# Rotary work in two jobs per tile, and full-height local queries, in an eight-stage two-layer network

## The chip, the cores and the metric

The kernel runs on one core of one Trainium2 chip. The metric is the device time of the whole program in microseconds (us). The engines are TensorE (PE, with its weight loads shown apart as PEld), VectorE (DVE), ScalarE (ACT), GpSimd (POOL) and SyncE (SP), which here only issues DMAs. A change of less than 0.2% (10 us) is about what a measurement of this kernel can not tell from none.

## What is computed

A residual stream x of shape (8, 512, 256), float32, goes through eight sublayers, each on the layer-normalised stream and added back: differential attention, mixture of experts, routed (local plus selected) attention, experts again, a selective state space, a block-quantised feed-forward, full attention, the same feed-forward. Two of them matter here.

```python
# differential attention, 16 half-heads of 16 channels, causal
q, k = rotary(rmsnorm(x @ Wq)), rotary(rmsnorm(x @ Wk))   # x1*c + x2*s, -x1*s + x2*c
att = softmax(q1 k1.T) v - lam * softmax(q2 k2.T) v       # per head, then a layernorm per head
y = ((1 - lam_init) * layernorm(att)) @ Wproj
# routed attention: 8 heads of 64 channels
light = softmax(mask + q_local @ k_window.T) v             # windows of 64 keys, three to a query
heavy = softmax(hq @ hk.T) hv                               # 256 picked queries, 256 picked keys
y = light @ wo_l + scatter(heavy @ wo_h)
```

## The kernel before

**Differential attention** (`diff_attention`, L143). The work is one software pipeline over 128 slots: 16 half-heads (NH) in each of 8 batches (B). Every engine walks the same slot numbers in program order; semaphores tie them together. In slot s PE computes the scores of softmax s+2 (L264, stationary operand 48 rows high), in even slots the values of a finished pair (L279, output in two 64-column halves), and then whatever "odd" jobs the hand-written `table` (L156) puts there: transposing x, projecting q and k (`qk`) and v, turning q and k (`turn`, L307), turning a head's output back (`back`), turning the attended rows (`heads`) and the output projection (`out`). A table entry (at, kind, i) is slot 16 b + at for batch b, so -17 is slot 15 of an earlier batch's sixteen. Odd jobs share three PSUM banks (NODD) in order; a bank must be emptied by ACT or DVE before the third next job may fill it. `vector_table`, `scalar_table` and `pool_table` (L160 to L166) place the jobs of the other engines; an engine empties in slot s what PE filled in slot s-1, before its own table jobs.

The rotary work of a tile t is one DVE job, `rope` (L477): multiply the 128x512 tile by the reciprocal norm (L478), drain and signal, wait for POOL's `swap` (L562) which multiplies the swapped halves with the sine (L569), multiply by the cosine in place (L482), drain, add POOL's half (L486). A `turn` job waits for all four tiles of its batch (L308), transposes four blocks (L310); ACT rounds the result to `hi` (L385), DVE subtracts to `lo` (L428), both in two buffers; ACT waits for the spill of the chunk two before (L384). SP writes hi and lo to DRAM with six DMAs a chunk (L245), four chunks a batch, and then issues some 20 DMAs of 512 KB that clear DRAM for the experts (`clear_regions`, L2734). POOL's `stack` jobs (L573, slots -9 and -1) wait for the spill and load it back into qT and kT, which the scores read. POOL also multiplies the causal triangle into each softmax (L546, L548). ACT computes the exponentials (L346), and once per batch two square roots, which need table loads.

When a head is done (`back` on DVE, L431 to L445), DVE takes the reciprocals of the eight row sums (L435), multiplies four of them by -lambda (L437), multiplies both halves (L438, L440) and adds them (L445), with a drain after each step.

**Routed attention** (`routed_attention`, L1134) is the same kind of pipeline over 192 slots: 8 batches, 4 chunks of two heads, 4 light and 2 heavy softmaxes a chunk. `scores` (L1233): for a light one a bf16 matmul adds the mask to the bank (L1242), then two matmuls of 256 columns (L1254) contract 64 rows, partitions 0 to 63 or 64 to 127 by the head's parity `par`, of q and k (L1249, L1250) or of the tile hqk (L1252, L1253). Then come `turn` (four transposes of the softmax of slot s-1, L1265), in every second slot `values` (L1291), and odd jobs in two banks. ACT copies q and k out of PSUM (L1447) and both halves of hqk in one copy (L1452), each releasing its bank after a drain. Before the pipeline a prologue on DVE (L1577 to L1600) sets constants and signals `s_ready`, on which POOL and PE wait.

## Time and profile before

| what | before |
|---|---|
| median of 3 runs | 4904.13 us (4897.9 to 4906.65) |
| the profiled execution | 4896.55 us |
| its span, first to last instruction | 4894.8 us |
| PE busy in the span | 3919.6 us (80%) |
| DVE / ACT / POOL busy | 2934.8 / 1749.0 / 1554.0 us |
| mean granted PE clock | 0.892 of full |
| differential attention, about | 35 to 670 us |
| routed attention, about | 1250 to 2108 us |

The profiled execution's own time exceeds its span by 1.75 us; it lies 7.6 us (0.15%) below the median of the runs. Busy time is the union of an engine's instructions; ends of matmuls are modelled, so the distance from one start to the next says more than a duration does. A float32 matmul shows as two records.

### The profile page before, as it was taken

How to read it: one execution, taken by the hardware profiler on the slowest of the kernel's cores; microseconds unless marked ns; L12 is line 12 of the kernel's file. 1: busy time of each engine (PE TensorE's matmuls, PEld its weight loads, DVE VectorE, ACT ScalarE, POOL GpSimd, SP SyncE). 2: the span in 40 equal slices, each digit the busy share in tenths (PEclk: the TensorE clock that was granted, in tenths of full speed). 3: DMA queues.
4: the chain of work that ended last, by engine and by line, in shares of the span. 5: the costliest groups of instructions: out<-in, count | busy, mean ns of one | idle time of the engine just before them, and what ended most of it. 6: DMA issues, size and time to landing. Idle time of an engine off the chain costs nothing. (4 is left out here: it accounts for less than half of the span.)

```text
span 4894.8 us, 59730 instructions
## 1 busy us (share of the span) xinstructions
PE 3919.6 (80%) x19240; PEld 2599.4 (53%) x19240; DVE 2934.8 (60%) x5538; ACT 1749.0 (36%) x3490; POOL 1554.0 (32%) x1463
## 2 busy tenths in 40 slices
PE   2888877994599999987993677774887788888888
PEld 2555556883477777766883334342554233333555
DVE  4566656664544445456664556556897466664898
ACT  2555543441344443443441232322111255545111
POOL 2555525445555444435445000000000433430000
PEclk7898988997799999988997788887998699998999
DMA  4988902553100000002554100000000544440000
GB/s 123 262 215 240 260 24 84 163 170 114 34 1 1 1 1 1 1 28 89 165 165 141 32 0 0 0 0 13 0 0 1 108 88 94 92 91 14 9 13 13
DMA packets 222619, 348.69 MB, mean 71 GB/s; under 512 B 34136, under 2 KB 127258, under 8 KB 216218
## 3 DMA queue, kind: packets, MB, share of 16 engines
q1 hardware_dynamic: 199706, 261.27, 17.7%
q0 software_dynamic: 22656, 84.24, 7.9%
q8 instruction: 131, 2.15, 0.2%
q14 instruction: 126, 1.03, 0.1%
HBM read 166.90 MB, written 169.87 MB: 69 GB/s over the span
## 5 line engine op out<-in xcount | busy, mean ns | idle before, releaser
L2532 DVE TENSOR_REDUCE ab_nmx<-banks 128x1 f32<-128x512 f32 x512 | 334.9, 687 | 226.8 <-PE banks L2348 226.0
L2586 POOL DMA_DIRECT2D ab_kT<-in_ab_ones x4 | 2.1, 535 | 1072.6 <-POOLq L2737 1072.6
L1620 POOL TENSOR_TENSOR lb_pq<-lb_pq,lb_rr 128x512 f32<-128x512 f32 x192 | 201.6, 1053 | 424.1 <-DVE lb_rr L1519 421.5
L2474 ACT ACTIVATE ab_pt<-banks 128x512 f32<-128x512 f32 x512 | 273.8, 600 | 94.8 <-PE banks L2358 83.0
L1514 DVE TENSOR_REDUCE lb_nmx<-banks 128x2 f32<-128x512 f32 x192 | 132.1, 688 | 278.1 <-PE banks L1254 277.1
L1402 ACT ACTIVATE lb_pq<-banks,lb_nmx 128x256 f32<-128x256 f32 x384 | 178.9, 471 | 301.0 <-DVE lb_nmx L1514 300.9
L2358 PE MATMUL banks<-ab_qT,ab_kT 49*128 49x512 f32 x512 | 232.1, 501 | 56.5 <-ACT ab_pt L2474 51.7
L2348 PE MATMUL banks<-ab_kT,ab_qT 48*128 48x512 f32 x512 | 239.6, 517 | 30.3 <-DMA ab_kT<-ab_spill 19.2
L2358 PEld LDWEIGHTS banks<-ab_qT,ab_kT 49*128 49x128 f32 x512 | 94.1, 198 | 271.9 <-ACT ab_pt L2474 158.7
L279 PE MATMUL banks<-da_pt,da_vx 128*64 128x512 f32 (+3 forms) x1024 | 183.5, 508 | 0.0
L346 ACT ACTIVATE da_pt<-banks 128x512 f32<-128x512 f32 (+1 forms) x384 | 174.9, 535 | 13.7 <-PE banks L264 12.6
L264 PE MATMUL banks<-da_qT,da_kT 48*128 48x512 f32 (+3 forms) x512 | 132.2, 377 | 40.9 <-ACT da_pt L346 32.1
L546 POOL TENSOR_TENSOR da_pt<-da_pt,w_da_tri 128x384 f32<-128x384 f32 x128 | 133.8, 1045 | 77.3 <-ACT da_pt L346 76.9
L1000 DVE CAST moe_a_h_hi<-moe_a_h_raw 128x512 fp32r<-128x512 f32 x124 | 88.6, 714 | 112.9 <-ACT moe_a_h_raw L873 112.0
L2369 PE MATMUL banks<-ab_pt,ab_vx 128*32 128x512 f32 x1024 | 152.7, 672 | 0.0
L1000 DVE CAST moe_b_h_hi<-moe_b_h_raw 128x512 fp32r<-128x512 f32 x124 | 85.8, 692 | 110.5 <-ACT moe_b_h_raw L873 109.6
L1084 POOL TENSOR_TENSOR moe_a_w_lo<-moe_a_w_raw,moe_a_w_hi 128x1024 fp32r<-128x1024 f32 x48 | 115.7, 2415 | 114.5 <-ACT moe_a_w_hi L880 106.8
L1084 POOL TENSOR_TENSOR moe_b_w_lo<-moe_b_w_raw,moe_b_w_hi 128x1024 fp32r<-128x1024 f32 x48 | 115.6, 2413 | 102.3 <-ACT moe_b_w_hi L880 94.9
L138 PE MATMUL banks<-moe_b_w_hi,moe_b_h_hi 128*128 128x256 f32 x496 | 143.8, 290 | 3.2 <-DVE residual L1029 3.2
L138 PE MATMUL banks<-moe_a_w_hi,moe_a_h_hi 128*128 128x256 f32 x496 | 143.7, 290 | 3.2 <-DVE residual L1029 3.2
L1254 PE MATMUL banks<-lb_k,lb_q 64*128 64x256 f32 x512 | 144.3, 402 | 0.0
L138 PE MATMUL banks<-moe_b_w_lo,moe_b_h_hi 128*128 128x256 f32 x496 | 141.5, 285 | 0.0
(534 smaller groups left out, 11347.9 us busy)
## 6 DMA issues: line engine op xcount, KB each, us to landing
moe_xs<-zero SPq DMA_DIRECT2D x71, 512.0 KB, 11.0
moe_ys<-zero SPq DMA_DIRECT2D x71, 512.0 KB, 11.8
moe_a_w_raw<-in_moe_w SPq DMA_DIRECT2D x48, 512.0 KB, 3.7
moe_b_w_raw<-in_moe_w SPq DMA_DIRECT2D x48, 512.0 KB, 3.7
da_spill<-da_hi SPq DMA_DIRECT2D x128, 128.0 KB, 2.4
ab_spill<-ab_hi SPq DMA_DIRECT2D x128, 128.0 KB, 2.4
da_qT<-da_spill POOLq DMA_DIRECT2D x32, 384.0 KB, 6.9
da_kT<-da_spill POOLq DMA_DIRECT2D x32, 384.0 KB, 10.6
```

The lines of the kernel that those rows point to most:

```text
L138: done = core.nc.tensor.matmul(bank, a[i], b[j], start=(first and n == 0), stop=(last and n == len(terms) - 1))
L279: last = nc.tensor.matmul(ps[64 * sub:64 * sub + 64, AV_BANK + hv % 2, j * P:T], vx[b % 2][:, j, h, :], pt[:, (2 * hv + sub) % RING, c0:c0 ...
L346: nc.scalar.activation(pt[:, n % RING, c0:c1], ps[:, S_BANK + (3 * n + u) % 3, 0:c1 - c0], ACT.Exp, scale=1.0 / math.sqrt(DA_D)).then_inc( ...
L1000: nc.vector.tensor_copy(h_parts[0][:, n % 2, m, :], h_raw[:, m % 2, :])
L1084: nc.gpsimd.tensor_tensor(parts[1][:, l % 2, :, :], raw[:, :, :], parts[0][:, l % 2, :, :].bitcast(F32), ALU.subtract).then_inc(done, 1)
L1402: nc.scalar.activation(pq[:, n % RING, t, :], ps[:, S_BANK + n % 2, 2 * P * t:2 * P * t + 2 * P], ACT.Exp, bias=nmx[:, n % RING, t:t + 1], ...
L1620: nc.gpsimd.tensor_tensor(pq[:, n % RING, :, :], pq[:, n % RING, :, :], bcast(rr[:, n % RING, :], 2, 2 * P), ALU.mult).then_inc(s_p, 1)
L2348: nc.tensor.matmul(ps[:, MAX_BANK + n % 3, :], qT[b % 2][r:r + AB_ROWS, p, qt * P:(qt + 1) * P], kT[b % 2][r:r + AB_ROWS, p, :], start=Tru ...
L2358: nc.tensor.matmul(ps[:, EXP_BANK + n % 3, :], kT[b % 2][r:r + AB_ROWS + 1, p, j * P:(j + 1) * P], qT[b % 2][r:r + AB_ROWS + 1, p, :], sta ...
L2369: last = nc.tensor.matmul(ps[32 * i:32 * i + 32, SUM_BANK, :], vx[b % 2][:, j, h + i, :], pt[:, (4 * v + i) % RING, :], start=(j == 0), st ...
L2474: nc.scalar.activation(pt[:, s % RING, :], ps[:, EXP_BANK + s % 3, :], ACT.Exp, scale=AB_D ** -0.5).then_inc(s_e, 1)
L2532: nc.vector.tensor_reduce(nmx[:, g % 2, col:col + 1], ps[:, MAX_BANK + n % 3, :], op=ALU.max, axis=AX.X, negate=True).then_inc(s_mx, 1)
```

## The change

In differential attention the `rope` job is split: `scaled` holds the first multiplication and signals POOL without a drain, `rope` the rest. Tiles 0 and 1 are scaled in slot -20, tiles 2 and 3 in -19, the `rope` jobs lie in slots -18 and -17, the swaps one slot later than before for three of the tiles. The v projections move one slot earlier and ahead of the turns; the turns move to slots -14, -13, -12, -11, one in each. In `back` the small multiplication with -lambda and a drain go, and the last sum becomes t2 * (-lambda) + t1 in one instruction. In routed attention q and the picked queries get a copy per head parity, whose other 64 partitions are zero; the score matmuls contract all 128 partitions.

```diff
-             (-17, "turn", 0), (-16, "turn", 1), (-15, "v", 0), (-14, "turn", 2), (-14, "v", 1), (-13, "turn", 3),
+             (-16, "v", 0), (-15, "v", 1), (-14, "turn", 0), (-13, "turn", 1), (-12, "turn", 2), (-11, "turn", 3),
...
-                    (-20, "rms", 0), (-20, "rope", 0), (-19, "rope", 1), (-19, "rope", 2), (-18, "rope", 3),
+                    (-20, "rms", 0), (-20, "scaled", 0), (-20, "scaled", 1), (-19, "scaled", 2), (-19, "scaled", 3),
+                    (-18, "rope", 0), (-18, "rope", 1), (-17, "rope", 2), (-17, "rope", 3),
...
-                  (-20, "swap", 0), (-19, "swap", 1), (-19, "swap", 2), (-18, "swap", 3),
+                  (-19, "swap", 0), (-19, "swap", 1), (-18, "swap", 2), (-17, "swap", 3),
...
-                        nc.vector.tensor_scalar(rr[:, r, :, 1:2], rr[:, r, :, 1:2], nlam[:, :], None, ALU.mult)
                         nc.vector.tensor_tensor(t1[:, :, :], sums[:, :, 0, 0:32], bcast(rr[:, r, :, 0], 2, 32), ALU.mult)
-                        dve.drain()
...
-                        nc.vector.tensor_tensor(att[:, b % 2, :, i, :], t1[:, :, :], t2[:, :, :], ALU.add)
+                        nc.vector.scalar_tensor_tensor(att[:, b % 2, :, i, :], t2[:, :, :], nlam[:, :], t1[:, :, :],
+                                                       ALU.mult, ALU.add)
...
+                def scaled(b, t):
+                    nc.vector.tensor_tensor(groups(qk[:, t, :]), groups(qk[:, t, :]),
+                                            bcast(srcp[:, t, :].rearrange("p (c r) -> p c r", r=4), 2, DA_D), ALU.mult).then_inc(s_qn, 1)
+
                 def rope(b, t):
-                    nc.vector.tensor_tensor(groups(qk[:, t, :]), groups(qk[:, t, :]),
-                                            bcast(srcp[:, t, :].rearrange("p (c r) -> p c r", r=4), 2, DA_D), ALU.mult)
-                    dve.drain().then_inc(s_qn, 1)
                     dve.wait_ge(s_swap, NT * b + t + 1)
...
-        q, k = sb("q", [P, 2, T]), sb("k", [P, 2, LB_TP])
+        q, k = sb("q", [P, 2, 2, T]), sb("k", [P, 2, LB_TP])
...
-        hqk = sb("hqk", [P, 2, 2, LB_SEL])
+        hq, hk = sb("hq", [P, 2, 2, LB_SEL]), sb("hk", [P, 2, LB_SEL])
...
-                            mine = q[r0:r0 + LB_D, c, qt * P:qt * P + P]
-                            keys = k[r0:r0 + LB_D, c, qt * P:qt * P + 2 * P]
+                            mine = q[:, c, par, qt * P:qt * P + P]
+                            keys = k[:, c, qt * P:qt * P + 2 * P]
                         else:
-                            mine = hqk[r0:r0 + LB_D, c, 0, t * P:t * P + P]
-                            keys = hqk[r0:r0 + LB_D, c, 1, :]
+                            mine = hq[:, c, par, t * P:t * P + P]
+                            keys = hk[:, c, :]
...
-                        dst = q[:, chunk % 2, :] if kind == "q" else k[:, chunk % 2, LB_W:LB_W + T]
-                        nc.scalar.copy(dst, bank).then_inc(s_qk, 1)
+                        if kind == "q":
+                            nc.scalar.copy(q[0:LB_D, chunk % 2, 0, :], bank[0:LB_D, :])
+                            nc.scalar.copy(q[LB_D:P, chunk % 2, 1, :], bank[LB_D:P, :]).then_inc(s_qk, 1)
+                        else:
+                            nc.scalar.copy(k[:, chunk % 2, LB_W:LB_W + T], bank).then_inc(s_qk, 1)
...
-                        nc.scalar.copy(hqk[:, chunk % 2, :, :],
-                                       bank.rearrange("p (r n) -> p r n", r=2)).then_inc(s_hqk, 1)
+                        nc.scalar.copy(hq[0:LB_D, chunk % 2, 0, :], bank[0:LB_D, 0:LB_SEL])
+                        nc.scalar.copy(hq[LB_D:P, chunk % 2, 1, :], bank[LB_D:P, 0:LB_SEL])
+                        nc.scalar.copy(hk[:, chunk % 2, :], bank[:, LB_SEL:2 * LB_SEL]).then_inc(s_hqk, 1)
...
+                for x in (q, hq):
+                    nc.vector.memset(x[LB_D:P, :, 0, :], 0.0)
+                    nc.vector.memset(x[0:LB_D, :, 1, :], 0.0)
```

## Rows read from the trace of the kernel before

**Rows 1.** Busy time by stretch: length, then busy us per engine, PE clock, DMA, GB/s

```profile
120.00:590.00 470.00, 403.46 (x2144) 250.34 (x2143) 292.78 (x527) 251.22 (x507) 261.00 (x335) 0.88 0.88 245
1296.00:2108.00 812.00, 808.19 (x4671) 587.42 (x4671) 389.05 (x893) 353.21 (x1055) 384.39 (x340) 1.00 0.00 1
```

**Rows 2.** Waits of PE, 35 to 665 us: us in total, times, longest

```profile
PE banks L310 <- DVE da_qk L486: 66.0, 8, 20.6
```

**Rows 3.** Timeline of PE, one batch of differential attention: start, length

```profile
255.61 1.08 PE L310 MATMUL banks<-ident,da_qk 128*128 128x128 f32 x4 [5.69 <-DVE da_qk L486]
...
264.36 0.90 PE L264 MATMUL banks<-da_qT,da_kT 48*128 48x512 f32 x4
...
265.60 0.36 PE L138 MATMUL banks<-da_wv_hi,da_xT_hi 128*128 128x256 f32 x1
...
267.20 0.91 PE L264 MATMUL banks<-da_qT,da_kT 48*128 48x512 f32 x4
268.04 2.38 PE L279 MATMUL banks<-da_pt,da_vx 128*64 128x512 f32 x16
```

**Rows 4.** Timeline of DVE and POOL around the rotary work of one batch

```profile
306.87 0.69 DVE L478 TENSOR_TENSOR da_qk<-da_qk,da_srcp 128x512 f32<-128x512 f32 x1
...
307.67 1.26 POOL L569 TENSOR_TENSOR da_rot<-da_qk,w_da_sin 128x512 f32<-128x512 f32 x1 [6.79 <-DVEq L480]
...
308.89 1.00 POOL L546 TENSOR_TENSOR da_pt<-da_pt,w_da_tri 128x384 f32<-128x384 f32 x1
308.96 1.47 DVE L482 TENSOR_TENSOR da_qk<-da_qk,w_da_cos 128x512 f32<-128x512 f32 x1 [1.41 <-POOL da_rot L569]
...
324.77 3.19 DVE L112 TENSOR_SCALAR x_normed<-residual,mean_var,rstd 128x256 f32<-128x256 f32 x4
```

**Rows 5.** The first batch: PE timeline, and first issue of POOL's loads

```profile
74.06 1.94 PE L310 MATMUL banks<-ident,da_qk 128*128 128x128 f32 x8 [20.65 <-DVE da_qk L486]
...
105.69 3.10 PE L264 MATMUL banks<-da_qT,da_kT 48*128 48x512 f32 x8 [8.70 <-DMA da_kT<-da_spill]
...
L580 POOL DMA_DIRECT2D da_qT<-da_spill x32: 506/542/714, 93.3 to 585.9; - x32
```

**Rows 6.** SP's spill issues, first and last of 24, and time to landing

```profile
76.52 0.51 SPq L245 DMA_DIRECT2D da_spill<-da_hi  x1
...
91.17 0.60 SPq L245 DMA_DIRECT2D da_spill<-da_lo  x1
...
DMA to landing us min/median/max: 2.2/2.4/4.1
```

**Rows 7.** The small multiplication on DVE: duration ns min/median/max

```profile
L437 DVE TENSOR_SCALAR da_rr<-da_rr,da_nlam x64: 229/264/2057, 144.3 to 645.3; 128x4 f32<-128x4 f32 x64
```

**Rows 8.** Timeline of PE in routed attention, around one light score

```profile
1600.08 0.39 PE L1242 MATMUL banks<-lb_maskb,lb_identb 128*128 128x512 bf16 x1
1600.40 1.13 PE L1254 MATMUL banks<-lb_k,lb_q 64*128 64x256 f32 x4
1601.45 0.66 PE L1265 MATMUL banks<-ident,lb_pq 128*128 128x128 f32 x4
1601.87 0.47 PE L138 MATMUL banks<-lb_xT_hi,lb_wqkv_hi 128*128 128x512 f32 x1
1602.18 0.39 PE L138 MATMUL banks<-lb_xT_lo,lb_wqkv_hi 128*128 128x512 f32 x1
1602.41 0.39 PE L138 MATMUL banks<-lb_xT_hi,lb_wqkv_lo 128*128 128x512 f32 x1
...
1618.19 1.03 PE L1347 MATMUL banks<-lb_gT,w_lb_wkvh 128*128 128x256 f32 x4
1619.06 0.38 PE L1242 MATMUL banks<-lb_maskb,lb_identb 128*128 128x512 bf16 x1
```

**Rows 9.** DVE in the prologue of routed attention

```profile
1253.77 0.30 DVE L1587 MEMSET lb_k<- 128x128 f32 x2
```

**Rows 10.** ACT's copies of q: duration ns min/median/max, first and last start

```profile
L1447 ACT COPY lb_q<-banks x32: 586/586/589, 1289.1 to 2079.5; 128x512 f32<-128x512 f32 x32
```

More of the change, by code:

```diff
@@ L515, in rescale @@
                     nc.vector.tensor_tensor(heads_of(b), heads_of(b), bcast(mean[:, :], 2, 32), ALU.mult).then_inc(s_ln, 1)
-                jobs_of = {"normal": normal, "xlo": low_x, "sum": sum_squares, "rms": rms, "rope": rope,
+                jobs_of = {"normal": normal, "xlo": low_x, "sum": sum_squares, "rms": rms, "scaled": scaled, "rope": rope,
                            "mean": mean_of, "centre": centre, "square": square, "var": variance, "scale": rescale}
@@ L1234, in scores @@
                     b, m, kind, i, par = of(n)
-                    r0, c = LB_D * par, (LB_FC * b + m) % 2
+                    c = (LB_FC * b + m) % 2
                     bank = ps[:, S_BANK + n % 2, :]
```

## The prediction

> **What bounds the kernel now.** I read the busy time by stretch first, because the change touches two of eight stages and an average over 4.9 ms says nothing about either. In routed attention PE is busy 808.2 of 812 us at full clock, while DVE, ACT and POOL are each below half [rows 1]. Whatever PE does there is paid in full, and only PE counts. In differential attention PE is busy 403 of 470 us in the steady part, at a mean clock of 0.88, with DVE at 293, POOL at 261 and ACT at 251 [rows 1]: no engine is full, so waits decide. The list of PE's waits names the largest, the first turn of each batch on the last rotary addition: 66.0 us in 8 times, 20.6 of it in the first batch [rows 2]. So 45.4 us belong to seven later batches, 6.5 us each. The timeline of one such batch shows the cost behind the wait: from the turn at 255.61 to the scores of the next slot at 264.36 PE needs 8.75 us [rows 3].
>
> **Routed attention, the score matmuls.** The change removes no column of work; what can go is the time around the 64-row matmuls. I read start to start. The mask starts at 1600.08 and the scores at 1600.40, 0.32 us; a matmul of the same 512 columns between full-height neighbours takes 0.23 (1602.18 to 1602.41). The scores to the transposes take 1.05 us; the same columns at full height take 0.87 (1618.19 to 1619.06). The transposes to the projection and on to its second matmul take 0.42 + 0.31, where the 0.31 would be 0.23. Lost: 0.09 + 0.18 + 0.08 = 0.35 us a score [rows 8]. A matmul at full height takes no longer per column, since the 0.87 is measured at 128 rows. There are 192 scores. Those that follow `values` directly, whose output lies in 64-column halves, keep part of the loss, so I take 0.33 us: 192 x 0.33 = 63 us gained. Bounds: 0.18, if only the step after the scores goes (35 us), and 0.36 (69 us). In the Trainium skill, TensorEngine Tiling (Array Packing), under Key Properties, a change of tiling mode drains TensorE; the gaps in the rows stand where such a change would be, so by that rule the loss goes, as summed. The other way, the page TensorE: Matmul & The Clock Gate, under Part 3, has small matmuls in distinct row groups run at the same time, which zeros would forfeit; by it the change would lose where two such neighbours stand. In this kernel both matmuls of a slot lie in the same row group and the other head's come a slot later, so nothing is forfeited.
>
> **Its side costs.** Four memsets, two of 1024 and two of 512 elements a partition, join DVE's prologue, where DVE runs without a pause up to the ready signal. Two memsets of 128 take 0.30 us together [rows 9], 1.17 ns an element; 3072 elements give 3.6 us, less for start-up: I take +3 us, bounds 0 and +4. ACT gets a second copy of q (586 ns, [rows 10]) and three shorter copies in place of the one of hqk, each shorter than 586: at most 32 x (0.59 + 2 x 0.59) = 56 us on an engine that is busy 353 of 812 [rows 1]. I cost it at nothing: PE has another bank to fill meanwhile, and exponentials are waited for two slots later. If that cover goes, each late bank costs up to 0.6 us; 64 of them bound it at +38, and I keep +10.
>
> **Differential attention, the steady part.** In the new order PE does in slots 0 and 1 what needs no rotary result (output projection, v), and turns only from slot 2 on. What is late next? DVE. Splitting the job looks as if POOL's swap (1.26 us) would now run beside DVE's multiplications. The rows speak against it: the cosine multiplication that starts while POOL's triangle runs takes 1.47 us, where the multiplication of the same shape at 306.87, with POOL still, takes 0.69. It ends 0.54 us after the triangle, so it stood still for most of it [rows 4]. I therefore leave the rotary chain as long as it is, 306.87 to 324.77, plus 3.2 for the normalisation that ends at 327.96 [rows 4]. The Trainium skill, SBUF — State Buffer, holds the port pair of DVE and GpSimd to be an exclusive lock, also for a VectorE operation with two SBUF inputs; that agrees, and a forecast with full overlap would put the chain near 12 us in place of 17.9.
>
> PE fills v's first half into the bank that DVE frees after its jobs of slot 15. Let T be the time at which PE now starts the turn, after standing for 5.7 us [rows 3]. It will fill these with scores (0.9), values (2.4, [rows 3]) and an output projection (four float32 matmuls of 256 columns, 2 x 0.87 [rows 8]): 5.0 us, so PE arrives at about T - 0.7. DVE now ends the normalisation at T + 3 [rows 4]; with fewer waits in between I give it T - 0.5 to T + 2.5 and take T + 1. With v at 1.6 us (265.60 to 267.20) the next slot starts at T + 2.6, against T + 8.75 [rows 3]. The work left behind differs by 0.5 us in favour of the new order. That is 6.6 us gained a batch, bounds 4 and 8.5.
>
> Something is given back. The turns now stand in four slots in a row and pass through two hi/lo buffers. SP issues a chunk's six DMAs in (91.77 - 76.52) / 4 = 3.8 us, and they land after 2.4 [rows 6]; with ACT's and DVE's 1.3 us that is 7.5 us from turn 0 until ACT may round turn 2. Slots 3 and 4 hold little, about 5.4 us. ACT stands there, with the exponentials queued behind it and PE's scores waiting for them. I take 2 us a batch, bounds 0 and 5. POOL's load job in slot -9 has still two slots to spare. The swaps one slot later wait for what DVE has by then done, so POOL's triangles lose nothing. SP starts its clearing DMAs about two slots later; it waits longer than that before each batch's first chunk. Sum: 7 x (6.6 - 2) = 32 us gained, bounds 0 and 60.
>
> **The first batch.** There the chain to the first scores is bare: turns at 74.06, POOL's loads at 93.3, scores at 105.69 [rows 5]. The v projections and x of the next batch no longer stand behind ACT's wait for the first spill, so that the next batch's qk, which POOL's square and with it the loads are queued behind, comes earlier. The walk: first spill issued at about 75.6 (a little earlier than 76.5), second chunk landed 2 x 3.8 + 2.4 later, at 85.6 [rows 6]; ACT then rounds turn 3 (0.6) and copies the first qk, which PE has ready by then, POOL squares it (1.1), and with the signals between them the loads go out at about 88.5, against 93.3. That is 5 us gained, bounds 0 and 9.
>
> **The second softmax's factor.** 64 small multiplications of 264 ns (up to 2057 beside POOL) and 64 drains go [rows 7], 17 us by the median. DVE waits for PE's `back` most of the time, so it is worth nothing on the path, at most 5 us; the fused sum replaces one of equal size.
>
> **Sum.** -63 + 3 - 32 - 5 = -97. Against the profiled execution, 4896.55, that is 4799.5. That execution lies 7.6 us under the median of 4904.13; splitting the difference, **I predict 4804 us**.
>
> **The rivals.**
> *A, the clustered turns and the DVE/POOL exclusion eat the whole gain of differential attention's steady part.* For it: the 7.5 us against 5.4, and the 1.47 us cosine [rows 4, 6]. Against it: PE need not wait for the rotary work at all in slots 15 and 0. Time: -63 + 3 - 5 = -65, 4832, with the same offset 4836. Chance 0.12. The lock of the SBUF page is the reason such a case has a chance at all.
> *B, full-height matmuls don't remove the gaps* (they come from loading float32 weights, not from the height; the change then doesn't do what it says). For it: after the v halves a first float32 matmul is slow too. Against it: full-height scores would stand between full-height neighbours, and 0.87 is measured there [rows 8]. Time: +3 - 37 = -34, 4866. Chance 0.08.
> *C, slower.* ACT's wait for the spill two chunks back grows, because the DMA queue still carries clearing traffic (DMA busy 0.88, [rows 1]) when the denser turns come; exponentials and scores stall. Everything else sums to -63 + 3 - 46 - 5 = -111, so it decides from 111 / 7 = 16 us a batch; at 18 us a batch the time is 4916. Against it: landings are 2.2 to 4.1 us even now [rows 6]. Chance 0.03, with 0.01 for other slow ends.
> *The forecast's case* has 0.73, and 0.03 is left for sums near zero.
>
> **Range and chances.** The bounds of the forecast's own case give -134 (69 + 60 + 9 less 4) to about -45; cutting the ends that need every bound at once, and reaching to rival A, I give 4768 to 4848. A change of 0.2% (10 us) is about what the measurement can tell. Faster: 0.73 + 0.12 + 0.08 = 0.93; same 0.03; slower 0.04.
>
> **What would show it.** Right: PE's wait at L310 for the rotary addition gone but for the first batch; in routed attention scores to transposes 0.87 us, mask to scores near 0.23, the stage about 60 us shorter with PE still full; the rotary chain on DVE no shorter than 17 us. Wrong: PE waiting at v (L138) or at the scores for ACT (L346) by more than 4 us a batch; the 1.05 us unchanged at 128 rows; ACT or a bank release appearing among PE's waits of routed attention.

## The result and the profile after

The changed kernel takes 4814.13 us (median of 4 runs, 4808.16 to 4830.99), the kernel before beside it 4903.94: a ratio of 0.9827, 95% interval 0.9815 to 0.984. The forecast was 4804 in a range of 4768 to 4848. The profiled execution is the longest of the four, 4830.99 us, so stages are compared here and totals by the medians.

| stage, by its first and last instruction | before | after | difference | forecast |
|---|---|---|---|---|
| start to first differential scores | 105.7 | 98.3 | -7.4 | -5 |
| first to last differential scores | 524.5 | 507.8 | -16.7 | -32 |
| routed set-up, DVE's first write of lb_s (L1579) to first row maximum | 44.3 | 47.4 | +3.1 | +3 |
| routed attention, first to last row maximum | 810.8 | 748.9 | -61.9 | -63 |
| full attention, not touched, first to last exponential | 629.6 | 643.4 | +13.8 | 0 |

The set-up is measured from an instruction of DVE's prologue that lies ahead of the memsets and of the ready signal, so the memsets are in it. The last row is no effect of the change: in the twelve profiles below, all with the same code in that stage, it took 617.3 to 640.0 us, and the time goes with the granted clock there, 0.90 on average in this profile and 0.94 in the one of 617.3 us. It explains most of why this one profile is longer than its kernel's median.

Busy time by stretch of the changed kernel (length, busy us per engine, TensorE clock, DMA share, GB/s), the stretches moved with the stages:

```profile
120.00:573.00 453.00, 392.93 (x2105) 250.62 (x2101) 281.27 (x475) 241.55 (x491) 267.28 (x328) 0.89 0.88 252
1267.00:2020.00 753.00, 741.85 (x4628) 613.28 (x4690) 382.45 (x887) 385.87 (x1145) 381.71 (x340) 1.00 0.00 1
```

Against [rows 1] routed attention is shorter with PE still full (741.9 of 753) and still at a granted clock of 1.00, while ACT rose only to 386 of 753: PE bounds the stage as before and simply has less to do. The weight loads rose from 587 to 613 us although the stretch shrank. The steady differential stretch looks the same as before.

In routed attention, the timeline of PE around one light and one heavy score:

```profile
1599.97 0.60 PE L1266 MATMUL banks<-ident,lb_pq 128*128 128x128 f32 x4
1600.33 0.36 PE L138 MATMUL banks<-lb_wqkv_hi,lb_xT_hi 128*128 128x256 f32 x1
...
1602.49 1.03 PE L1255 MATMUL banks<-lb_k,lb_q 128*128 128x256 f32 x4
1603.35 0.60 PE L1266 MATMUL banks<-ident,lb_pq 128*128 128x128 f32 x4
...
1619.96 1.03 PE L1255 MATMUL banks<-lb_hk,lb_hq 128*128 128x256 f32 x4
1620.82 0.60 PE L1266 MATMUL banks<-ident,lb_pq 128*128 128x128 f32 x4
```

Scores to transposes, start to start, is 0.86 us in both; it was 1.05 [rows 8], and the medians over 189 scores are 0.86 and 1.06. The transposes to the next work take 0.36 in place of 0.42, and a mask to its scores 0.22 (1652.50 to 1652.72) in place of 0.32. Same columns, same clock, less time around them.

In differential attention the waits of PE from 0 to 700 us (us in total, times, longest):

```profile
PE banks L265 <- ACT da_pt L347: 31.2, 21, 3.1
PE banks L138 <- DVE residual L448: 25.0, 5, 5.3
PE banks L311 <- DVE da_qk L487: 15.3, 1, 15.3
...
PE banks L138 <- DVE da_t L439: 6.1, 1, 6.1
```

The 66.0 us at the turn [rows 2] are down to 15.3, all in the first batch. In its place PE waits at the v projection: 25.0 + 6.1 us in six of the seven later batches. So 45.4 us of later waits became 31.1. The timeline of PE, POOL and DVE in the batch around 300 us says why:

```profile
294.09 1.05 POOL L581 DMA_DIRECT2D da_qT<-da_spill  x2
295.14 1.00 POOL L581 DMA_DIRECT2D da_kT<-da_spill  x2
296.15 1.28 POOL L570 TENSOR_TENSOR da_rot<-da_qk,w_da_sin 128x512 f32<-128x512 f32 x1
296.88 1.99 PE L327 MATMUL banks<-w_da_wo,x_normed_T 128*128 128x256 f32 x8
297.39 1.00 POOL L547 TENSOR_TENSOR da_pt<-da_pt,w_da_tri 128x384 f32<-128x384 f32 x1
297.47 3.23 DVE L483 TENSOR_TENSOR da_qk<-da_qk,w_da_cos 128x512 f32<-128x512 f32 x1 [2.78 <-POOL da_rot L570]
...
303.45 0.68 DVE L448 TENSOR_TENSOR residual<-banks,residual 128x512 f32<-128x512 f32 x1
...
304.19 0.58 PE L138 MATMUL banks<-da_wv_hi,da_xT_hi 128*128 128x256 f32 x1 [5.31 <-DVE residual L448]
```

PE ends the output projection at 298.87 and waits 5.31 us for the bank that L448 frees. DVE is late because its last cosine waits 2.78 us for POOL's last swap, and the swap stands behind the four load issues of the "stack" jobs, 2.05 us together (0.5 each), in the slot to which the change moved it. The cosine then takes 3.23 us, with POOL's triangles beside it. And after the wait v runs slowly, 2.86 us from 304.19 to the next scores at 307.05, where it took 1.6 in [rows 3].

The whole rotary chain of that batch, from DVE's first scaling to its last addition, is the second measure of this. DVE's timeline, the changed kernel first, then loads_late (an experiment below, with those load issues one slot later):

```profile
281.84 4.97 DVE L478 TENSOR_TENSOR da_qk<-da_qk,da_srcp 128x512 f32<-128x512 f32 x4
...
300.78 1.32 DVE L487 TENSOR_TENSOR da_qk<-da_qk,da_rot 128x512 f32<-128x512 f32 x1
```

```profile
279.83 4.96 DVE L478 TENSOR_TENSOR da_qk<-da_qk,da_srcp 128x512 f32<-128x512 f32 x4
...
295.97 0.79 DVE L487 TENSOR_TENSOR da_qk<-da_qk,da_rot 128x512 f32<-128x512 f32 x1
```

That is 20.3 us in the changed kernel and 16.9 in loads_late; before it was 18.0 (306.87 to 324.85). In the fourth to the eighth batch it is 17.9 to 18.0 us in the two profiles with the code of before, 20.2 to 21.1 in the five of the changed code, and 16.3 to 17.4 in the three with the change and the later loads. So the change made the chain over 2 us longer.

Three short stretches of the same profile show the clock:

```profile
295.00:300.00 5.00, 3.88 (x24) 2.30 (x20) 2.53 (x1) 0.70 (x2) 4.98 (x8) 1.00 1.12 351
...
307.00:310.00 3.00, 3.00 (x12) 2.53 (x12) 1.16 (x9) 2.44 (x5) 0.17 (x1) 0.50 0.28 94
...
312.00:314.00 2.00, 2.00 (x11) 1.08 (x12) 0.00 (x0) 1.72 (x4) 0.00 (x0) 1.00 0.00 0
```

The granted clock is 1.00 up to the wait, 0.50 (1.2 in place of 2.4 GHz) after it, with PE fully busy, and 1.00 again from about 312 (the stretch from 310 to 312 reads 0.55).

### The profile page after: what moved, and what is told of

Same layout as the page of the kernel before. It is cut to its first block and busy times, and to the rows that moved or that the text cites. A ratio compares the mean times of both kernels' runs of the same rounds, so it can differ in the third digit from the quotient of the medians.

```text
span 4829.2 us, 59607 instructions
## 1 busy us (share of the span) xinstructions
PE 3867.0 (80%) x19177; PEld 2634.5 (55%) x19240; DVE 2932.7 (61%) x5478; ACT 1780.3 (37%) x3586; POOL 1566.8 (32%) x1463
## 5 line engine op out<-in xcount | busy, mean ns | idle before, releaser
L347 ACT ACTIVATE da_pt<-banks 128x512 f32<-128x512 f32 (+1 forms) x384 | 174.7, 537 | 21.6 <-PE banks L265 19.6
L547 POOL TENSOR_TENSOR da_pt<-da_pt,w_da_tri 128x384 f32<-128x384 f32 x128 | 145.3, 1135 | 111.4 <-ACT da_pt L347 107.3
L280 PE MATMUL banks<-da_pt,da_vx 128*64 128x512 f32 (+3 forms) x1024 | 170.6, 480 | 1.1 <-POOL da_pt L549 1.1
L1085 POOL TENSOR_TENSOR moe_b_w_lo<-moe_b_w_raw,moe_b_w_hi 128x1024 fp32r<-128x1024 f32 x48 | 115.1, 2405 | 101.1 <-ACT moe_b_w_hi L881 94.8
L138 PE MATMUL banks<-moe_b_w_hi,moe_b_h_hi 128*128 128x256 f32 x496 | 143.7, 290 | 3.2 <-DVE residual L1030 3.2
L138 PE MATMUL banks<-moe_a_w_hi,moe_a_h_hi 128*128 128x256 f32 x496 | 143.2, 289 | 3.2 <-DVE residual L1030 3.2
L138 PE MATMUL banks<-moe_b_w_lo,moe_b_h_hi 128*128 128x256 f32 x496 | 141.3, 285 | 0.0
L138 PE MATMUL banks<-moe_b_w_hi,moe_b_h_lo 128*128 128x256 f32 x496 | 141.1, 285 | 0.0
## 6 DMA issues: line engine op xcount, KB each, us to landing
moe_ys<-zero SPq DMA_DIRECT2D x71, 512.0 KB, 10.9
```

The costliest lines, as they stand in the source:

```text
L138: done = core.nc.tensor.matmul(bank, a[i], b[j], start=(first and n == 0), stop=(last and n == len(terms) - 1))
L280: last = nc.tensor.matmul(ps[64 * sub:64 * sub + 64, AV_BANK + hv % 2, j * P:T], vx[b % 2][:, j, h, :], pt[:, (2 * hv + sub) % RING, c0:c0 ...
L347: nc.scalar.activation(pt[:, n % RING, c0:c1], ps[:, S_BANK + (3 * n + u) % 3, 0:c1 - c0], ACT.Exp, scale=1.0 / math.sqrt(DA_D)).then_inc( ...
L1085: nc.gpsimd.tensor_tensor(parts[1][:, l % 2, :, :], raw[:, :, :], parts[0][:, l % 2, :, :].bitcast(F32), ALU.subtract).then_inc(done, 1)
```

## The experiments

Twelve runs, four on each of three chips, in the order of the table. On the second and third chip the expert stages, which no edit touches, take longer (the first of them, from first to last instruction on the tile moe_a_xr, 589 to 595 us, against 578 to 581), so ratios are to the kernel before on the same chip, whose medians were 4906.23, 4928.75 and 4929.78 us, and stages are compared as above.

| run | median us | ratio to before, 95% | first scores | their stretch | routed set-up | routed |
|---|---|---|---|---|---|---|
| after_again | 4827.46 | 0.9846 (0.9819 to 0.9873) | 98.1 | 515.8 | 47.7 | 748.8 |
| routed_only | 4843.53 | 0.9871 (0.984 to 0.9903) | 103.8 | 522.6 | 47.7 | 749.2 |
| da_only | 4894.36 | 0.997 (0.9953 to 0.9988) | 98.2 | 509.2 | 44.4 | 810.7 |
| all_half | 4873.02 | 0.9947 (0.9926 to 0.9967) | 97.4 | 511.9 | 47.8 | 811.2 |
| split_only | 4873.08 | 0.9894 (0.9865 to 0.9922) | 101.8 | 534.2 | 47.7 | 749.1 |
| turns_only | 4839.55 | 0.9817 (0.9789 to 0.9846) | 101.1 | 502.5 | 47.3 | 749.2 |
| loads_late | 4819.18 | 0.9776 (0.9743 to 0.9809) | 95.9 | 484.6 | 47.7 | 749.1 |
| loads_norm_late | 4813.93 | 0.9777 (0.9735 to 0.9818) | 97.4 | 486.6 | 47.7 | 749.0 |
| after_beside | 4861.45 | 0.9852 (0.9834 to 0.987) | 97.2 | 518.6 | 47.7 | 749.0 |
| loads_late_zeros | 4825.27 | 0.979 (0.9772 to 0.9808) | 99.0 | 489.4 | 44.0 | 749.1 |
| turns_loads_late | 4842.59 | 0.9815 (0.9793 to 0.9837) | 99.3 | 503.2 | 47.7 | 749.2 |
| da_height_mix | 4813.35 | 0.9768 (0.9744 to 0.9793) | 97.4 | 489.4 | 47.7 | 749.0 |

The scatter matters: five profiles with the changed code in differential attention have a stretch of 507.8 to 518.6 us (after, after_again, da_only, all_half, after_beside), two with the code of before 524.5 and 522.6.

**The change again, and its two halves.** routed_only takes back everything in differential attention, da_only everything in routed attention.

> The changed kernel once more, for a second profiled execution. Theory: its profile shows routed attention about 60 us and differential attention about 23 us shorter than before, and the 15 us that full attention took longer in the first profile are variation between executions and do not recur; time 4808 to 4820 us. Rival: the full-attention stage, which the change does not touch, is really 15 us longer in the changed kernel, and is so again.

> Only the routed-attention part of the change. Theory (the score matmuls lose about 0.35 us each to the change of height, the side costs are 3 us): first to last row maximum of the stage 810.8 to about 749 us, total 58 to 60 us under before, 4844 to 4846. Rival (the gain there is partly owed to an earlier or differently aligned start): clearly less than 58.

> Only the differential-attention part. Theory: 20 to 30 us under before, 4874 to 4884; PE's wait moves from the turn to the first v projection, about 5 us a batch, and most of the gain lies in the first batch and period. Rival (the two parts are not additive): a difference from before that with routed_only does not sum to that of the whole change within 10 us.

The stages separate cleanly: 748.8 to 749.2 us wherever the scores are full height, 810.7 with the old ones, whatever stands elsewhere. By ratio the routed half is worth 1.3%, the differential half 0.3%. da_only's first scores are 5.6 us earlier than routed_only's and 7.5 earlier than before's. The two halves add up: 62.7 and 11.9 us under before, 74.6 together, where the whole change is 78.8 under it. Full attention took 627.1 us in after_again, so the 643.4 of the first profile did not recur. Two of the expected totals missed: after_again came 7 us above its range (4827 for 4808 to 4820) and da_only 10 us above (4894 for 4874 to 4884), though its stages are 22 us shorter than before's (7.5 to the first scores, 13 to 15 in their stretch).

**Height or copies (all_half).** The padded tiles, copies and memsets stay; only the matmuls read 64 rows again.

```diff
-                            mine = q[:, c, par, qt * P:qt * P + P]
-                            keys = k[:, c, qt * P:qt * P + 2 * P]
+                            mine = q[LB_D * par:LB_D * par + LB_D, c, par, qt * P:qt * P + P]
+                            keys = k[LB_D * par:LB_D * par + LB_D, c, qt * P:qt * P + 2 * P]
```

(and the same for hq and hk)

> The changed kernel, but its score matmuls in routed attention read 64 rows again, from the same zero-padded tiles: copies, memsets and tiles stay, only the height of the matmuls goes back. Theory (the height is the whole gain): the stage is as long as before plus the side costs, total 60 to 66 us above the changed kernel, 4872 to 4882; the scores to the transposes take 1.05 us again. Rival (the separate tiles or the order of ACT's copies gave part of it): less than 50 us above the changed kernel.

The timeline of PE in all_half has the old gap back:

```profile
1602.48 1.13 PE L1255 MATMUL banks<-lb_k,lb_q 64*128 64x256 f32 x4
1603.54 0.66 PE L1266 MATMUL banks<-ident,lb_pq 128*128 128x128 f32 x4
```

1.06 us from scores to transposes, and 811.2 us for the stage, while ACT's extra copies are there and the set-up keeps its 47.8. The height alone is worth 62.2 us (811.2 - 749.0), 0.32 us a score for 192 scores. The totals say less: all_half is only 45.6 us above after_again, which by its number is what the rival said (less than 50) and not the 60 to 66 expected. The stages of the two profiled executions, 47.4 us apart, show where the rest went: routed attention is 62.4 us longer in all_half, full attention 9.8 shorter (617.3 to 627.1) and the differential scores 3.9, both with the same code. Rival B falls by the stage. What happens inside TensorE at a change of height no run shows.

**Split or order (split_only, turns_only).** split_only keeps the two rotary jobs and puts PE's turns and v back into the slots of before; turns_only keeps PE's new order and puts the rotary work of a tile back into one job, with the swaps in their old slots.

```diff
-             (-16, "v", 0), (-15, "v", 1), (-14, "turn", 0), (-13, "turn", 1), (-12, "turn", 2), (-11, "turn", 3),
+             (-17, "turn", 0), (-16, "turn", 1), (-15, "v", 0), (-14, "turn", 2), (-14, "v", 1), (-13, "turn", 3),
```

> The changed kernel with the old order of jobs on PE (turns 0 and 1 in the slots before and beside v, v in between), the rotary work still split in two jobs. My theory (the order of PE's jobs carries the gain of differential attention, the split nothing): PE waits at the turn for the rotary addition again, 5 to 7 us in each of the seven later batches and some 20 us in the first; first scores at about 104 us, the scores' stretch 518 to 526 us instead of 508 to 516; time 12 to 20 us above the changed kernel. Rival (the split shortens the rotary chain on VectorE by running POOL's swap beside the multiplications): the wait at the turn falls to 3 us a batch or less and the time is within 6 us of the changed kernel.

> The changed kernel with the rotary work in one job per tile, as before, in the old slots of VectorE and POOL, and the later turns kept. My theory: the wait stays at v, and since POOL's swaps are asked for a little earlier the wait at v is 3 to 6 us a batch; first scores near 98 us, the scores' stretch 505 to 516 us, time within 8 us of the changed kernel either way. Rival (the split is needed for the later turns to pay): the wait at v grows to 7 us a batch or more, the stretch is 520 us or longer, the time 10 us or more above the changed kernel.

The waits of PE, split_only:

```profile
PE banks L311 <- DVE da_qk L487: 73.3, 8, 18.8
```

and turns_only (its lines are those of its own listing, L279 the values, L551 the triangle):

```profile
PE banks L279 <- POOL da_pt L551: 29.1, 7, 4.7
```

The split without the later turns is no help: 73.3 us of waits at the turn against 66.0, a stretch of 534.2. My theory held in kind, but the loss is larger than it allowed: the stretch is 8 us above its bound, and the ratio is 0.4 to 0.7% above those of the changed kernel, 20 to 33 us. This run keeps the last swap in the slot of the load issues, and its rotary chain is 18.9 to 19.6 us in the later batches, against 18.0 before; so it prices the split together with that collision and not the split by itself. The later turns without the split gain at least as much as the whole change: 502.5, with nothing left at the turn but the first batch's 17.6. By ratio that is 5 to 17 us below the changed kernel, where I expected 8 at most. And I had the place of the remaining wait wrong. It is not at v but at the values, for POOL. The timeline of POOL in turns_only:

```profile
287.41 1.27 POOL L572 TENSOR_TENSOR da_rot<-da_qk,w_da_sin 128x512 f32<-128x512 f32 x1 [6.55 <-DVEq L483]
...
300.72 1.26 POOL L572 TENSOR_TENSOR da_rot<-da_qk,w_da_sin 128x512 f32<-128x512 f32 x1 [2.38 <-DVEq L483]
301.94 0.99 POOL L549 TENSOR_TENSOR da_pt<-da_pt,w_da_tri 128x384 f32<-128x384 f32 x1
302.89 0.90 POOL L551 TENSOR_TENSOR da_pt<-da_pt,w_da_tri 128x128 f32<-128x128 f32 x1
```

POOL stands at each swap until DVE has multiplied that tile, and the triangle that PE's values need is queued behind it. PE's values of that slot start at 303.85, after a wait of 4.45 us for L551. The split removes this wait (POOL finds its input ready) and puts the one at v in its place.

**The load issues (loads_late, loads_norm_late).** One number in POOL's table, and in the second run one in DVE's.

```diff
-                  (-9, "stack", 0), (-9, "stack", 1), (-1, "stack", 2), (-1, "stack", 3)]
+                  (-9, "stack", 0), (-9, "stack", 1), (0, "stack", 2), (0, "stack", 3)]
```

```diff
-    vector_table = [(-33, "normal", 0), ...
+    vector_table = [(-32, "normal", 0), ...
```

> The changed kernel with POOL's second pair of load jobs one slot later, so that its four DMA issues (1.0 us each with their waits) no longer stand ahead of the last swap of the next batch. My theory (the last swap comes late because it is queued on POOL behind the triangle and these issues): the wait at v for VectorE's residual falls from 5.3 to 3 to 3.5 us a batch, the scores' stretch gets 5 to 12 us shorter, the time 5 to 12 us. Rival (VectorE is late by its own work and its cosines that stand still beside POOL): the wait at v stays above 4.5 us and the time within 3 us. Second rival: the scores then wait for the keys that these loads bring, and the wait at the scores for a DMA grows from 10.6 us in all to 25 or more.

> The same, and VectorE's normalisation of the next x one slot later too, so that the residual that frees v's bank comes 1.5 us earlier on VectorE. My theory: the wait at v falls to 1.5 to 2.5 us a batch, the stretch of the scores is 10 to 18 us shorter than in the changed kernel, the time 8 to 18 us. Rival: what is taken from the wait at v comes back as PE's wait for the transposed x of the next batch or for VectorE at the next banks, and the time is within 4 us of the changed kernel.

The waits of PE in loads_late:

```profile
PE banks L138 <- DVE residual L448: 12.3, 4, 3.1
...
PE banks L265 <- DMA da_kT<-da_spill: 9.4, 1, 9.4
```

PE stalls once a batch at the same place, for ACT before the scores, and a batch can be measured from stall to stall. It takes 64.9 us here, 69.2 in the changed kernel and 70.0 before. Between the stalls four batches apart (235.50 to 515.30 before, 211.40 to 488.30 in the changed kernel, 213.30 to 472.75 in loads_late) all three execute the same 1280 matmuls. Busy time of these stretches (length, PE, PEld, DVE, ACT, POOL, clock, DMA, GB/s), in this order:

```profile
235.50:515.30 279.80, 237.04 (x1280) 148.57 (x1280) 190.34 (x341) 146.55 (x297) 155.90 (x196) 0.90 0.86 239
```

```profile
211.40:488.30 276.90, 239.25 (x1280) 155.19 (x1281) 183.91 (x309) 145.74 (x297) 163.77 (x196) 0.89 0.85 243
```

```profile
213.30:472.75 259.45, 230.25 (x1280) 147.88 (x1280) 184.63 (x309) 145.91 (x297) 164.19 (x196) 0.93 0.91 261
```

The wait at v fell from 5.3 to 3.1 us as my theory had it, and the keys came no later. (The four issues hold POOL for 2.05 us in all, 0.5 each, not the 1.0 each of my expectation.) But the stretch fell by more than the 5 to 12 us expected, 18 to 34 against the five profiles of the changed code, and in these four batches a batch got 4.4 us shorter, twice the wait. PE's idle time fell from 37.7 to 29.2 us, 2.1 a batch: that is the wait. Its busy time for the same work fell from 239.3 to 230.3, 2.2 a batch, with a higher granted clock (0.93 for 0.89). After the wait of 3.1 us the clock is back sooner here:

```profile
300.00:303.00 3.00, 2.49 (x11) 2.49 (x12) 2.74 (x9) 0.00 (x0) 1.12 (x2) 0.54 1.17 191
303.00:305.00 2.00, 2.00 (x13) 1.54 (x12) 1.22 (x8) 1.36 (x3) 0.00 (x0) 0.83 0.99 147
```

It is low for some 3 us (300.5 to about 303.7), in the changed kernel for some 7.5 (304.2 to about 312); 4 us more at half speed cost 2. The second half of this gain does not repeat. loads_late_zeros, below, has the same code and the same waits in this stage; the same 64 slots, and the stretch behind its wait of 3.1 us at 301.96:

```profile
213.10:480.60 267.50, 238.22 (x1280) 152.56 (x1280) 181.29 (x309) 145.99 (x297) 164.40 (x196) 0.90 0.88 255
...
308.00:314.00 6.00, 6.00 (x22) 3.71 (x22) 0.66 (x3) 1.95 (x4) 1.07 (x2) 0.50 0.00 1
```

PE is idle for 29.3 us, as in loads_late, but busy for 238.2, as in the changed kernel on its chip (238.4), and there the clock is at 0.50 until beyond 314 with PE fully busy. So the later loads are worth 2.1 us a batch by the wait (a batch is 66.9 us against 69.0 beside it), and how long the clock stays low behind a wait of the same length differs between executions. loads_norm_late lowers the wait at v to 2.1 us but not the stretch. The waits do not come back elsewhere, as its rival says: over the same 64 slots PE is idle for 25.1 us, 4 less than in loads_late, but busy for 242.1 at a granted clock of 0.89. Whether the edit or the execution has that low clock, one profile can't tell.

**Both edits beside the changed kernel on one chip (after_beside, loads_late_zeros).** The second run has loads_late's edit and the zeros written by POOL, which waits for the ready signal anyway:

```diff
@@ vector prologue
-                for x in (q, hq):
-                    nc.vector.memset(x[LB_D:P, :, 0, :], 0.0)
-                    nc.vector.memset(x[0:LB_D, :, 1, :], 0.0)
@@ gpsimd prologue, before its wait for the ready signal
+                for x in (q, hq):
+                    nc.gpsimd.memset(x[LB_D:P, :, 0, :], 0.0)
+                    nc.gpsimd.memset(x[0:LB_D, :, 1, :], 0.0)
+                pool.drain()
```

> The changed kernel again, on the chip of the three runs beside it, so that they can be held against it directly. Both theories expect a ratio to the kernel before of 0.982 to 0.986 and the stages as in its first profiles: first scores at 98 us, their stretch 508 to 516 us, routed attention's set-up 47.4 us.

> The changed kernel with POOL's second pair of load jobs one slot later and with the zeros of the local queries written by POOL, which waits for the stage's ready signal anyway, in place of VectorE. My theory (both costs are engine queues that work stands in, not work): routed attention's set-up returns from 47.5 to 44.3 us, the stretch of the differential scores is 20 us shorter or more, and the time is 18 to 30 us below the changed kernel on the same chip. Rival (the shorter stretch seen before came from the chip): the stretch is within 8 us of the changed kernel beside it and the time within 8 us. For the set-up, rival: the memsets on POOL hold up its own part of the set-up or VectorE's, and 47 us stay.

4825.27 against 4861.45 us, 36.2 less, more than the 18 to 30 expected: 29.2 in the stretch of the scores (518.6 to 489.4, the 518.6 being the longest of the five with the changed code), 3.7 in the set-up (47.7 to 44.0). The two profiled executions are further apart, 47.7 us, and 12.6 of that lies in full attention (630.4 and 617.8), which no edit touches. This version beats both kernels, 0.979 of the kernel before on its chip, and the two intervals (0.9772 to 0.9808, 0.9834 to 0.987) do not touch.

**Is the split worth anything once the loads are out of the way (turns_loads_late)?** turns_only's edit and loads_late's together.

> Rotary work in one job per tile as before, later turns, and POOL's second pair of load jobs one slot later. Theory one (the split is worth nothing in itself): the differential scores' stretch is within 5 us of that with the split and the same late loads, the time within 5 us apart from 3 us of set-up. Theory two (the split keeps POOL from standing at its swap for VectorE, with the triangles queued behind it): the stretch stays near the 502 us that one job per tile gave with the early loads, the values go on waiting 4 us a batch for POOL, and the time is 8 to 20 us above the split version.

Theory two. The stretch is 503.2, as with the early loads (502.5), and the wait at the values stays:

```profile
PE banks L279 <- POOL da_pt L551: 29.7, 7, 4.7
```

So the split and the late loads pay only together: 14 to 19 us more than one job per tile. Without the late loads the split gave nothing over one job per tile: 507.8 to 518.6 us against 502.5. That the late loads do nothing for one job per tile has a plain reason: there the last swap stands in slot 14, and the load issues in slot 15 never stood ahead of it. The rotary chains say the same: 17.7 to 18.7 us in turns_only and turns_loads_late, 16.3 to 17.4 with both edits. The split with its last swap alone moved back to slot 14 was not tried.

**Would full height help differential attention too (da_height_mix)?** There the scores contract 48 rows. The experiment reads all 128 rows of the query and key tiles, with zeros between the heads written once by POOL at the start, and so leaves out the separation of two heads, each score being the sum over both.

```diff
-                                                    kT[g][r:r + DA_ROWS, p, j * P:(j + 1) * P],
-                                                    qT[g][r:r + DA_ROWS, p, j * P:T], start=True, stop=True)
+                                                    kT[g][:, p, j * P:(j + 1) * P],
+                                                    qT[g][:, p, j * P:T], start=True, stop=True)
```

> The changed kernel with the scores of differential attention contracted over all 128 rows of the query and key tiles instead of one head's 48: each score is then a sum over two heads, so the kernel leaves out their separation, and its time shows what full height would be worth there; rows between the heads hold zeros, written once at the start. My theory (a change of height costs TensorE 0.3 us a score slot where it is the bound): 128 slots, less where PE waits anyway, so the stretch of the scores is 15 to 35 us shorter than in the changed kernel beside it. Rival (PE there waits for other engines, and the scores of one slot overlap by row groups or run on at one height): within 5 us, or longer.

The stretch is 29.2 us shorter than beside it (518.6 to 489.4) with the wait at v no shorter (27.0 us in 5, 25.1 in 5 beside it). The timeline of PE, first the changed kernel, then da_height_mix:

```profile
355.38 0.60 PE L316 MATMUL banks<-ident,da_osb 128*128 128x128 f32 x4
355.91 0.90 PE L265 MATMUL banks<-da_qT,da_kT 48*128 48x512 f32 x4
356.74 1.73 PE L280 MATMUL banks<-da_pt,da_vx 128*64 128x512 f32 x8
```

```profile
350.32 0.60 PE L316 MATMUL banks<-ident,da_osb 128*128 128x128 f32 x4
350.68 0.89 PE L265 MATMUL banks<-da_qT,da_kT 128*128 128x512 f32 x4
351.49 2.37 PE L280 MATMUL banks<-da_pt,da_vx 128*64 128x512 f32 x16
```

Transposes to scores is 0.36 us at 128 rows and 0.53 at 48; scores to the values, which are 64 wide in either case, 0.81 and 0.83. That is 0.19 us in this slot; as an estimate, for each of the 128 score slots, it makes 24 of the 29 us. Against all five profiles of the changed code the stretch is 18 to 29 us shorter, so the part of the height is less sure here than in routed attention. The size is a bound for a kernel that would place each head's queries with zeros beside them, as the change does in routed attention; such a kernel needs more memory for the queries and was not tried.

## Why the prediction was right, and where its terms were off

**Routed attention, -63: right, and by its mechanism.** The time around the 64-row matmuls goes: -61.9 in the first profile and 748.8 to 749.2 in every other with full height, against 810.7 to 811.2 at half height. 0.32 us a score where I took 0.33. The rows of a full-height pair elsewhere in the same stage were the right measure: 0.87 read there, 0.86 after.

**Its side costs, +3: right.** The set-up grew by 2.9 to 3.5 us, and went to 44.0 when POOL wrote the zeros. The memsets on DVE:

```profile
1228.77 0.91 DVE L1592 MEMSET lb_q<- 64x1024 f32 x1 [0.25 <-issue]
...
1231.61 0.48 DVE L1593 MEMSET lb_hq<- 64x512 f32 x1
```

From 1228.77 to 1232.07, where the next memset starts, is 3.3 us. ACT's copies at nothing: right. They are longer than I assumed from their size (64 rows take 581 ns, as long as 128), 33 us more busy time than before, and in all_half the stage is as long as before with all of them in it.

**The first batch, -5: right mechanism, a little small.** POOL's loads are first issued at 85.4 us (88.5 expected, 93.3 before), and the first scores start 7.4 us earlier, 5.6 against routed_only. split_only and turns_only lie between (101.8 and 101.1 us), so the order of PE's jobs, which my walk went by, is a part of it and not the whole.

**The steady part of differential attention, -32: wrong in size.** The five profiles of the changed code have a mean stretch of 512.7 us, the two of the old one 523.6: 10.9 us gained (4 to 17). The step that failed is the time at which DVE reaches v's bank, "T - 0.5 to T + 2.5", of which I took T + 1. In the new kernel T can't be read, since no turn stands there. If I set it so that PE arrives at T - 0.7 as forecast (298.87 in the batch shown), it is 299.6, and the bank came at 304.19, T + 4.6; without T, PE waited for 5.3 us where I had 1.7. I had gone through every queue for waits but not seen that the last swap, moved one slot later, lands in the slot in which POOL issues the second pair of loads; I wrote that "POOL's load job in slot -9 has still two slots to spare" and left out the one in slot -1, which is slot 15 of the batch. loads_late shows how much of it this is: with the loads one slot later the wait is 3.1 us, so the issues account for 2.2 of the 3.6 us by which DVE was later than I had it. The 1.4 that are left I can't divide; the cosine of 3.23 us lies there. With the loads later the stretch is 484.6 to 489.4 us, 18 to 34 us shorter, where 21 were missing; PE's waits at v are 16.4 us of that (31.1 in total to 14.7), and the rest is not traced beyond the clock, which differs between executions. A second part was not in the sum at all: I let v run in 1.6 us, as in [rows 3], where behind a wait of 5.3 us it takes 2.9, and the work behind v is slow for some 5 us more. In before the low clock lay behind the turn and was inside my 8.75 us; in the new order it lies behind v, and I had counted it as gone with the wait. Together: the next slot starts at T + 7.5 (307.05), where I had T + 2.6 and before it was T + 8.75. Over four batches (the rows above) PE is idle for 37.7 us in place of 42.8 and busy for 239.3 in place of 237.0, 0.7 us a batch gained of the 6.6 less 2 that I forecast (1.4 in da_only and all_half, where the same 64 slots take 274.3 us). In this profile the first 30 slots gain 16.7 us (129.8 to 113.1), the four batches 2.9, and the last 34 slots lose 2.9 (114.9 to 117.8). So what was gained was gained early, and the equal gain in seven batches that I forecast is not there; why the early batches gain so much I have not shown.

**The give-back of 2 us a batch: right on ACT, not there on PE.** ACT's rounding now waits for the spills,

```profile
ACT da_hi L386 <- DMA da_spill<-da_lo: 13.3, 8, 4.4
...
ACT da_hi L386 <- DMA da_spill<-da_hi: 8.4, 3, 3.3
```

21.7 us up to 700 us where it was 4.5. But PE's waits in the four batches are, before and after,

```profile
PE banks L310 <- DVE da_qk L486: 24.1, 4, 6.4
PE banks L264 <- ACT da_pt L346: 17.4, 12, 3.1
```

```profile
PE banks L138 <- DVE residual L448: 21.2, 4, 5.3
PE banks L265 <- ACT da_pt L347: 16.3, 12, 3.1
```

The wait for ACT's exponentials, where a give-back would show, is no longer than before. The spills cost PE nothing, and the wait moved from the turn to v almost whole: 24.1 to 21.2 us.

**The rotary chain no shorter: right as a bound, but it grew.** I left it at 17.9 us, and it became 20.2 to 21.1, 2.3 us or more longer, because of the load issues: with these later it is 16.3 to 17.4, some 1 us shorter than before. The lock of VectorE and POOL that [rows 4] suggested shows again: a multiplication of this shape takes 0.69 us where it is not held up [rows 4], the cosine above 3.23. By the Trainium skill, SBUF — State Buffer, this is the exclusive port pair; the trace agrees, since POOL works without a pause from 297.39 to beyond 300 while that cosine runs. My sign of being wrong here did come: PE waits at v (L138) for more than 4 us a batch.

**Rivals.** A came nearer in size than my own sum (0 for the steady part, 32 forecast, 10.9 measured) and had, in one half, the right cause: most of the steady gain is gone, but not through the clustered turns; through POOL's queue, with the lock and the clock behind it. B is refuted by all_half. C did not occur: the spills cost ACT 21.7 / 8 = 2.7 us a batch, a sixth of the 16 from which it decides, and PE nothing. By the Trainium skill, TensorEngine Tiling (Array Packing), Key Properties, a change of tiling mode drains TensorE; the 0.32 us a score of all_half and the 0.19 us a slot of da_height_mix agree with that. The sum came to -77 by stages (-61.9 + 3.4 - 7.4 - 10.9), the medians to -90, and -79 and -68 when the same kernel was measured again, against -97. So that the median came within 10 us of 4804 is in part luck: by stages the change is worth 20 us less than forecast, and the first comparison came out 11 to 22 us better than the later ones. The low end of the range is also not what its bounds give: 35 for the matmuls, nothing in differential attention and 4 of side costs are 31 us gained (21 with ACT's 10), where I wrote about 45.

## What to carry to other kernels

Where TensorE is full, price a matmul of fewer rows between full ones by start-to-start distances and compare them with a full-height pair elsewhere in the same stage: here the switch costs 0.2 to 0.3 us each time, and zeros in the unused rows are cheaper. When a job is moved one slot later on an in-order queue, list everything in the slot that it lands in, DMA issues too: four of them, 2 us a batch, made the chain 2 us longer in place of 1 us shorter and took most of the gain. Two edits that each give nothing alone (the split, the later loads) can be worth 14 to 19 us together, because one clears what the other runs into; so undo and redo them in pairs. When one number says yes and the other no, as in all_half, compare the stage that was edited and then find the stages that account for the rest.

## What the runs showed of the hardware that I had not expected

- A copy on ACT of 64 partitions and 512 elements takes 581 ns, one of 128 partitions 586: half the rows save nothing.
- A wait of PE costs more than its length, and by an amount that differs. In the batch shown the granted clock stayed at 0.50 for some 7.5 us of full work behind 5.3 us of wait; behind 3.1 us it did so for some 3 us in loads_late and for over 12 (301.96 to beyond 314) in loads_late_zeros, with the same code.
- Code that is the same in every kernel took from 617.3 to 643.4 us in full attention, at granted clocks of 0.94 and 0.90, more than a quarter of what the whole change is worth; only stages, not single totals, could be compared.
